# The start of a two-stage layer kernel: batch one's step size on another engine, its state weights in other tiles, and a new order of the queues

## The reference

```
x = layernorm(x + mixer(x));  x = layernorm(x + experts(x))
mixer:   z = x Wz;  B, C, dt_raw, X = split(x Win);  delta = softplus(dt_raw + dt_bias)
         h_t = exp(-delta_t exp(A_log)) h_{t-1} + X_t (delta_t B_t);   y_t = h_t C_t + D X_t
         out = (y * (silu(z) Wzg)) Wout              # 8 heads of 64, state size 64
experts: three routers x P_w^T U_r^T, top 3 of 12, softmax -> dw1, dw2, dw3
         h = gelu(sum_e dw1[e] W1[e] x);  y = sum_e dw2[e] W2[e] h + dw3 b2
```

## Time and profile before

| | |
|---|---|
| median of three runs | 1564.96 us (1563.9 to 1566.89) |
| the profiled execution | 1565.38 us |
| its span | 1563.7 us |
| TensorE busy | 1545.0 us, 99% |
| VectorE, ScalarE, POOL busy | 1108.0, 598.1, 663.7 us |
| chain of waits, by engine | TensorE 92%, POOL 4%, the rest 1% and less |
| DMA | 114.79 MB |

### The profile page before, as it was taken

One profiled execution on the slowest core, in us unless ns is written; L12 is line 12 of the kernel. 1 busy time (PEld: TensorE's weight loads), 2 busy tenths in 40 slices (PEclk: granted clock), 3 DMA queues, 4 the chain that ended last, 5 costly groups with the idle time before them and its releaser, 6 DMA issues.

```text
span 1563.7 us, 25298 instructions
## 1 busy us (share of the span) xinstructions
PE 1545.0 (99%) x8634; PEld 1249.2 (80%) x8634; DVE 1108.0 (71%) x3108; ACT 598.1 (38%) x1362; POOL 663.7 (42%) x755
## 2 busy tenths in 40 slices
PE   8999999999999999999999999999999999999998
PEld 6778788888888878888788888878888788887876
DVE  7577676877768687676776768777686776867755
ACT  6652424425144351533425244242443515335130
POOL 7681623616145270643616336162451715436040
PEclk9999999999999999999999999999999999999999
DMA  5350312304023040321403123040230403214020
GB/s 176 102 158 22 116 41 66 98 29 132 19 76 88 29 135 14 103 69 46 118 17 118 44 66 98 29 128 22 71 93 29 136 14 99 73 40 125 15 74 7
DMA packets 81600, 114.79 MB, mean 73 GB/s; under 512 B 10160, under 2 KB 37312, under 8 KB 81472
## 3 DMA queue, kind: packets, MB, share of 16 engines
q1 hardware_dynamic: 81472, 113.18, 24.9%
HBM read 108.02 MB, written 5.13 MB: 72 GB/s over the span
## 4 chain that ended last, share of the span: by engine, by line
PE 92%; POOL 4%; issue 1%; DVE 1%; DMA 1%; ACT 0%; SPq 0%; POOLq 0%; DVEq 0%; ACTq 0%
PE exp_bank L246 22%; PE exp_bank L248 22%; PE exp_bank L247 22%; PE mix_bank L893 4%; PE mix_bank L919 3%; PE mix_bank L246 3%; PE mix_bank L247 3%; PE mix_bank L248 3%; PE mix_bank L901 3%; PE mix_bank L790 1%; PE turn_bank L1224 1%; POOL w_lo L445 1%; PE mix_bank L738 1%; POOL Wt L853 1%; PE mix_bank L1010 1%
## 5 line engine op out<-in xcount | busy, mean ns | idle before, releaser
L1167 POOL TENSOR_TENSOR sp_lo<-fbuf,sp_hi 128x512 fp32r<-128x512 f32 (+2 forms) x203 | 246.6, 1218 | 179.3 <-ACT sp_hi L1164 112.7
L246 PE MATMUL exp_bank<-w_hi,sp_hi 128*128 128x512 f32 x768 | 307.5, 400 | 0.8 <-POOL sp_lo L1217 0.8
L246 PE MATMUL exp_bank<-sp_hi,w_hi 128*128 128x512 f32 x764 | 304.9, 399 | 2.2 <-POOL sp_lo L1167 2.0
L248 PE MATMUL exp_bank<-w_hi,sp_lo 128*128 128x512 f32 x768 | 303.2, 395 | 0.0
L247 PE MATMUL exp_bank<-w_lo,sp_hi 128*128 128x512 f32 x768 | 303.1, 395 | 0.0
L248 PE MATMUL exp_bank<-sp_hi,w_lo 128*128 128x512 f32 x764 | 300.5, 393 | 0.0
L247 PE MATMUL exp_bank<-sp_lo,w_hi 128*128 128x512 f32 x764 | 298.8, 391 | 0.0
L1264 DVE SCALAR_TENSOR_TENSOR acc<-exp_bank,dw,acc 128x128 f32<-128x128 f32 x384 | 132.2, 344 | 152.9 <-PE exp_bank L248 152.2
L1164 ACT CAST sp_hi<-fbuf 128x512 fp32r<-128x512 f32 (+2 forms) x203 | 120.0, 591 | 277.2 <-DVE fbuf L1134 217.2
L853 POOL TENSOR_TENSOR Wt<-Wt,Gh 128x512 f32<-128x512 f32 x128 | 184.9, 1446 | 23.0 <-DVE Wt L845 22.9
L246 PEld LDWEIGHTS exp_bank<-sp_hi,w_hi 128*128 128x128 f32 x764 | 143.6, 188 | 43.2 <-issue 8.0
(11 more groups left out here) (267 smaller groups left out, 2281.4 us busy)
## 6 DMA issues: line engine op xcount, KB each, us to landing
row_b<-dw_rows SPq DMA_DIRECT2D x190, 256.0 KB, 3.4
seg_b<-dA_rows SPq DMA_DIRECT2D x124, 256.0 KB, 3.6
ctd<-cum_rows SPq DMA_DIRECT2D x128, 96.0 KB, 3.3
x_in<-in_x SPq DMA_DIRECT2D x16, 256.0 KB, 2.8
result<-acc SPq DMA_DIRECT2D x15, 256.0 KB, 2.3
fbuf<-in_W1T SPq DMA_DIRECT2D x12, 256.0 KB, 4.2
acc<-in_W2T SPq DMA_DIRECT2D x5, 256.0 KB, 4.0
x_in<-in_W2T SPq DMA_DIRECT2D x3, 256.0 KB, 4.4
```

What stands on the lines that cost most here:

```text
L246: nc.tensor.matmul(ps, s_hi, m_hi, start=start and j == 0, stop=False)
L248: last = nc.tensor.matmul(ps, s_lo, m_hi, start=False, stop=stop and j == n - 1)
L1167: sig("xw_lo", PO.tensor_tensor(lo[:, cols], wide[e % 2][:, cols], hi[:, cols].bitcast(F32), ALU.subtract))
```

## The change

All of it lies in the setup, in the start and in the functions that they call. What it does:

- Batch one's step size (mix_step) runs on VectorE, in two halves with the mask copies between; the unit copy into PSUM moves from VectorE to ScalarE, ahead of everything. wzg_lo is made before the silu products.
- Batch one's state weights lie in zg (Xde0) instead of Wt. Its scans wait for the silu rests and the unit copy and no longer for the state matmuls; the copy of the first gate tile waits for the state matmuls instead.
- Batch two's xT_lo moves from VectorE to POOL. TensorE transposes batch two's x before batch one's scores.
- Weights: tiles 0 and 1 are cast on ScalarE, and their rests taken on VectorE later; tiles 2 and 3 get their rests on POOL, after a wait for the first ctd product. The others move in the queues of ScalarE and POOL, and their loads in that of SP.
- SP sends the rates, waits for that to land, reads rows 0 and 1, and only then sends the cumulative product.
- Batch two's step size: its first half on POOL comes before three rests of weights and its second half after them; its reciprocal on VectorE comes after the residual sum (L924) instead of before the last gate product; on ScalarE it comes after the tanh.
- VectorE's normalisation waits for the weights up to tile 8, ScalarE's x1T for those up to tile 9, and the logits copy for all twelve.
- TensorE: the rates of batch one come before X2 and X3; the states after the first gate tile; batch two's dt matmuls after y of the second pair; 29 filler matmuls fewer.

```
-        N1, NHP, LO_V = 12, 2, (0, 1, 2, 3)
+        N1, LO_V = 12, (0, 1)
@@ mix_x
-            if eng is DVE:
-                wait(DVE, "xT", b)
...
+            if eng is (PO if early else DVE):
+                wait(eng, "xT", b)
@@ mix_decay
-                wait(DVE, "ps_st", b)
+                if first(b):
+                    DVE.wait_ge(sems["unit"], 1)
+                    wait(DVE, "silu_lo", b)
+                else:
+                    wait(DVE, "ps_st", b)
@@ start_pe
-            mix_X(PE, b, range(4))
+            mix_X(PE, b, range(2))
...
             mix_rates(PE, b)
             mix_ends(PE, b)
+            mix_X(PE, b, range(2, 4))
+            mix_x(PE, nxt, True)
             router_product(PE)
-            keep_busy(rb, 6)
             mix_scores(PE, b)
-            keep_busy(rb, 12)
-            mix_states(PE, b)
-            mix_x(PE, nxt, True)
...
-            mix_zg(PE, b)
+            mix_zg(PE, b, range(1))
+            mix_states(PE, b)
+            mix_zg(PE, b, range(1, 3))
             mix_y_skip(PE, b, 0)
             mix_y(PE, b, 0)
             mix_y_skip(PE, b, 1)
+            mix_zg(PE, b, [3])
+            mix_y(PE, b, 1)
             mix_dt(PE, nxt)
-            mix_y(PE, b, 1)
+            mix_y_skip(PE, b, 2)
             mix_bc(PE, nxt)
-            mix_y_skip(PE, b, 2)
             mix_y(PE, b, 2)
             mix_z(PE, nxt)
             mix_y_skip(PE, b, 3)
             mix_y(PE, b, 3)
-            keep_busy(rb, 6)
+            keep_busy(rb, 3)
             mix_out(PE, b)
             mix_X(PE, nxt, range(2))
-            keep_busy(rb, 14)
+            keep_busy(rb, 6)
@@ start_dve
+            mix_step(DVE, b, on=DVE, parts=(0,))
             setup_masks(DVE)
-            split_w(DVE, range(0, 2))
-            mix_step(DVE, b)
+            mix_step(DVE, b, on=DVE, parts=(1,))
+            setup_zg(DVE)
             mix_z(DVE, b)
-            mix_X(DVE, b, range(2))
-            mix_silu_split(DVE, b, on=DVE)
+            mix_X(DVE, b, range(3))
             DVE.wait_ge(sems["zero"], 16)
             mix_rates(DVE, b)
-            setup_zg(DVE)
-            mix_X(DVE, b, range(2, 4))
-            split_w(DVE, range(2, 4))
+            mix_silu_split(DVE, b, on=DVE)
+            mix_X(DVE, b, [3])
             router_product(DVE)
+            split_w(DVE, range(2))
...
-            mix_step(DVE, nxt)
             mix_y(DVE, b, NQ - 1)
             mix_z(DVE, nxt)
             mix_out(DVE, b)
+            mix_step(DVE, nxt)
             route_stats(DVE, b)
+            first_weights_ready(DVE, 8)
+            route_scale(DVE, b)
             first_weights_ready(DVE)
-            route_scale(DVE, b)
@@ start_pool
-            neg_a_ready(PO)
-            mix_step(PO, b)
+            PO.wait_ge(sems["cast"], NCAST)
             skip_tables(PO)
             mix_ends(PO, b)
-            split_w(PO, range(4, 6))
             for q in range(NQ):
                 mix_decay(PO, b, 2 * q)
                 mix_decay(PO, b, 2 * q + 1)
-                if 0 < q < NQ - 1:
-                    split_w(PO, [5 + q])
-            mix_step(PO, nxt)
-            split_w(PO, range(8, 12))
+                if q == 0:
+                    wait(PO, "ctd", b, 1)
+                split_w(PO, ([2, 3], [4], [5], [])[q])
+                if q == 0:
+                    mix_x(PO, nxt, True)
+            mix_step(PO, nxt, parts=(0,))
+            split_w(PO, range(6, 9))
+            mix_step(PO, nxt, parts=(1,))
+            split_w(PO, [9])
             load_b2(PO)
             wait(PO, "x1", b)
+            split_w(PO, range(10, 12))
```

More of the change, by code:

```diff
@@ L349, in setup @@
                 AC.preload_act_table_set(LOG_EXP)
+                AC.wait_ge(sems["ident"], 2)
+                AC.copy(unit[:, :], ident4[:, :]).then_inc(sems["unit"], 1)
                 AC.wait_ge(sems["pad"], 5)
@@ L433, in split_w @@
                 at, landed, n = w_stage(k)
-                if k < NHP:
-                    if eng is DVE:
[L436 to L439, removed]
+                if eng is AC:
                     AC.wait_ge(landed, n)
@@ L531, in mix_dt @@
                 wait(AC, "ps_st", b.prev())
-                AC.copy(B_tok[:, :, :], ps[:, :, 0:NS])
-                wait(AC, "G_dt", b.prev())
+                if not first(b):
+                    AC.copy(B_tok[:, :, :], ps[:, :, 0:NS])
+                    wait(AC, "G_dt", b.prev())
                 sig("dt_raw", AC.copy(delta[:, :, :], ps[:, :, NS:NS + H]))
+                if first(b):
+                    AC.copy(B_tok[:, :, :], ps[:, :, 0:NS]).then_inc(sems["B_first"], 1)
         def mix_step(eng, b, on=PO, table=True, parts=(0, 1)):
@@ L615, in out_rows, with mix_z @@
                 out[bass.ds(b.index(), 1), :, :].rearrange("o (c p) d -> p (o c) d", p=P)
[L617 to L619 removed]
+        def mix_z(eng, b, ks=range(NK)):
+            for k in ks:
                 if eng is PE:
@@ L667, in mix_zg @@
                     wait(AC, "ps_out", b.prev())
+                    if first(b):
+                        wait(AC, "ps_st", b)
                     sig("zg", AC.copy(zg[:, q, :], bank_of(f"zg{q}", b)[:, :]))
@@ L749, in mix_ends @@
                 ps = bank_of("rates", b)
-                for part, first in ((a_hi, True), (a_lo, False)):
+                for part, opens in ((a_hi, True), (a_lo, False)):
                     PE.matmul(ps[:, P:P + (NC - 1) * H], strict_r[:, :], part[:, 0:NC - 1, :].rearrange("p c h -> p (c h)"),
-                              start=first, stop=not first)
+                              start=opens, stop=not opens)
                 sig("ps_ends", PE.matmul(ps[:, P + 64:P + 64 + NC * H], upper[:, P - 1:P].to_broadcast([P, P]),
@@ L1530, in start_act @@
             mix_ends(AC, b)
+            mix_silu_split(AC, b, on=DVE)
             mix_bc(AC, b)
-            split_w(AC, range(2, 6))
+            split_w(AC, range(2))
             mix_scores(AC, b)
```

83 lines of the change are left out of this document (46 added, 37 removed).

## The result

| | before | after |
|---|---|---|
| median of 20 runs each, in turns | 1565.45 us (1562.72 to 1567.41) | 1567.55 us (1564.26 to 1571.98) |
| ratio after to before | | 1.0018, 95% interval 1.001 to 1.0026 |
| profiled execution, its span | 1565.38, 1563.7 us | 1564.99, 1563.3 us |

The changed kernel is slower by about 2 us, and its median lies outside the range of 1560.6 to 1565.3. Two facts have to be held apart. The execution that was profiled is as long as the one of before; and the executions of the changed kernel do not agree with each other. Of its 20, ten took 1564.3 to 1566.9 us at a mean granted clock of 0.994 to 0.996, and ten 1568.2 to 1572.0 us at 0.991 to 0.993. The profile shows one of the first ten.

A forecast was written before the change was run, and what follows sets the result against it. POOL's chain from 9 to 57 us was taken to set the first expert matmul's start; 1.9 us earlier plus 0.4 of clock made 2.3, so 1563.1 from 1565.38 (1562.7 from the median), range 1560.6 to 1565.3.

The forecast's parts named there:

- Steps 1 to 5: From batch one's step size to the normalised x: gate 1.75 us earlier, residual sum done at 52.0, normalised x 2.2 earlier.
- step 1: Batch one's step size on VectorE, at 0.3 us an operation: done at 14.4 us, 3.0 before POOL's 17.46.
- Step 3: First ctd at 29.4; POOL waits for it, then takes rests and x rest: only 0.5 of 2.6 us left.
- Step 5: Gate at 46.75, 1.75 us earlier; residual sum at 52.0; L960's wait falls by 0.8, so normalised x comes 2.2 earlier.
- step 2: VectorE up to the first scan, weight and silu rests charged 1.8 and 1.9 beside POOL: scan at 23.8, 2.6 us earlier.
- Step 6: POOL's rests end at 59.8 and release the logits copy, 1.5 us earlier; ScalarE's copy of G ends 1.9 earlier.
- Step 7: Low-clock stretch comes earlier, over logits and scores, hidden by POOL's 59.8; the X matmul gets back 0.4 us.
- rival B: The new 3.2 us TensorE hole before y of the second pair costs 1.7 us of clock: 1564.4; chance 0.2.
- C: Rival: same hole, clock low until the last y; over the whole 10.8 us costs 5.4, 1568.1 us; chance 0.08.
- D: Rival: gain lost behind 72 us if late weights do not move with the rest: 1565.0 us; chance 0.07.
- A: Rival: less collision on VectorE than charged, cheaper rests and steps, whole 0.7 of clock back: 1561.4 us; chance 0.25.

The follow-up runs named there:

- a_nine: Changed kernel with measured fillers, reciprocal ahead of the residual sum, and tile 9's rest on VectorE instead of POOL; 1562.46 us, ratio to before 0.9979.
- a_tuned: Changed kernel with fillers measured to its holes (10, 2, 11, 18 and 3), reciprocal left behind the residual sum; 1563.78 us, ratio to before 0.9986.
- b_fill: Kernel before with fillers measured to its own holes (11, 3, 9, 18 and 3), nothing of the change; 1563.08 us, ratio to before 0.9985.
- a_r12: a_tuned with POOL's rests of tiles 12 and 13 taken in only 4 of 512 columns; 1562.57 us, ratio to before 0.9984.
- a_again: The changed kernel itself, run again without any edit; 1569.98 us, ratio to before 1.0022.
- a_hole11: Changed kernel with 11 fillers in the hole before y of the second pair, no other edit; 1565.76 us, ratio to before 1.0.
- a_late: Changed kernel with the earlier fillers around the output product given back (6 and 14 instead of 3 and 6); 1566.96 us, ratio to before 0.9999.

## Why the prediction was wrong

**Steps 1 to 5, up to the residual sum: right as a whole.** Predicted and measured, in us: a_lo 14.4 and 14.16; first scan 23.8 and 23.13; first ctd 29.4 and 29.15; y of the second pair done 37.8 and 37.73; gate 46.75 and 46.88; residual sum done 52.0 and 52.19. The two weight rests beside POOL cost 2.27 (L439), 0.5 more than the 1.8 charged, and the pair of silu rests, also beside POOL's state weights, 1.26 instead of 1.9, so not every such overlap stalls VectorE; POOL's tables took 2.03 instead of 3.74 and its state weights 4.86 instead of at most 4.0. That these errors cancel is luck. The steps had a pitch of 0.3 as taken (0.19 of it work for most); the lower bound of step 1 adds up to 12.3 and not 12.8, which changes nothing. Step 3's claim, that of a scan 2.6 us earlier little arrives because POOL takes on the x rest, holds: the scan came 3.3 earlier, y of the second pair 1.2.

**Step 5, the normalisation, mis-sized.** L975 started at 55.27, as forecast (57.57 - 2.2 = 55.4). But L975 was carried over at its 1.11 us, with POOL's rest of tile 9 newly beside it: 2.44. The prediction named that POOL's tiles would follow the reciprocal and asked only who waits for their end, not who runs beside them. It had charged exactly this at step 2, from the rests of the earlier trace rows, and left it out here. In a_nine the collision is worth 0.8 us.

**Step 6, "POOL decides again": right only at an even clock, and short in range.** POOL's last rest of the first set ended at 60.31 instead of 59.8. In the profile after, the logits matmuls ended later than that (61.10), as they ran at 1.2 GHz, and it was they that released the copy; POOL's rest released only ScalarE's cast of a late tile, at 60.34. The same eight took 1.1 us before. The group of TensorE's logits matmuls, 56 to 62 us:

```profile
L1019 PE MATMUL exp_bank<-router,fbuf 128*128 128x36 f32 x8 | 1.9, 410 | 0.8 <-ACT fbuf L1011 0.8
```

With the clock up (a_tuned) they end in time and the copy starts at 60.40, when POOL is done. Behind that, step 6 took "a stretch that had 8.4 us" over unchanged. That is the largest single term of the even-clock sum: the stretch from the logits copy to the first expert matmul grew from 9.54 us (b_fill) to 10.54 (a_tuned), because the rests of tiles 12 and 13 fall on the comparisons: with them short (a_r12) it is 9.63.

**Step 7, the clock: failed, and it decides the sign.** The prediction let the late low stretch move to where POOL hides it and give back 0.4. It came earlier (58.5 against 61.1), but lasted twice as long (6.8 against 3.4 us), over logits, scores and the first X. The early low stretch (14.2 to 21.1) was not foreseen; it was hidden behind VectorE, whose first scan starts at 23.13 with it and at 23.14 without (a_tuned). And the hole before the second pair's y, to which the sum gave nothing and rival B one stretch of 3.4 us with a chance of 0.2, costs 3.1 us at the last y in the profile of a_again. That about half of the first 20 executions fell there is inferred from their times. Rival B compared two holes of one profiled execution, and held it against the risk that TensorE stood from 11.9 to 14.9 at a granted 1.00. In the profile after, it stood 2.38 us in that place, up to 14.41, and the clock fell at 14.2, in a_again only at 16.0. So a hole can cost in one execution and not in the next, and one profile cannot show that.

**The rivals.** B named the place, and its price was for half the low time found; C's mechanism, a low clock until near the last y, is nearer: 36.6 to 43.4, about 60% of its 10.8 us. The executions of the slower kind took 1568.2 to 1572.0, at or above its 1568.1; that the median of all, 1567.55, comes so near to C's price is luck, for it lies between two kinds. Both together had 0.28, and the slower side only 0.04. The Trainium skill (TensorE: Matmul & The Clock Gate, HAM oscillation) states that idle gaps put the array back to half rate each time anew; the runs agree for three of the five profiles with this hole unfilled, and for the late one in every profile that had the change's few fillers there. D is refuted: from the first expert matmul to the end of the span it is 1491.7 us before and 1490.8 after, and 1490.0 to 1492.7 in all the kernels here. A is refuted too: there was more collision, not less.

**The sum, with what the runs showed in its place:** a lead of 1.9 us at the residual sum (against b_fill; 1.6 against the profile of before, where 1.8 was forecast), less 0.6 at the normalisation, less 0.1 at the logits, less 1.0 in the routing, leaves 0.2 at even clock. On top of that the change opens holes which cost it some 4 us (1567.55 against 1563.78 with all of them filled), where the holes of the kernel before cost 2.4 (1565.51 against 1563.08). The difference of the two is the result. By place, the middle hole alone is worth 1.8 to 2.8 us (a_hole11) and the late ones alone 3.0 (a_late against a_again); these are of different groups of runs and need not add up to the whole.

## What to carry to other kernels

When work moves from a saturated helper engine to another, list what will then run beside each short operation on the path, and charge every one of them up to a whole instruction of the other engine. Where a change drops filler or makes a new wait on TensorE, measure several executions of it and compare their mean clocks before believing the profile of one; and before pricing any change near a hole, fill the holes of the kernel before, which here alone was worth as much as the change was meant to bring.

## What the runs showed that was not expected

- The granted clock after one and the same hole of 2.69 us stayed at 1.00 in one execution of a kernel and went to 0.50 in another. The low stretches seen lasted 3.4 us (61.1 to 64.6 before), 6.8 (14.2 to 21.1 and 58.5 to 65.4 after, 36.6 to 43.4 in a_again) and 10.2 (60.5 to 70.7 in a_again).
- A VectorE operation of 128x4 elements, 0.16 us elsewhere, stood for 1.16 us until POOL's rest of 1.29 us was over. MAX8 on 128x12, which has one input, did not stall: the twelve of batch one took 0.96 us beside POOL's rests, and all 192 of the kernel before lie between 0.153 and 0.176 us each.
- More work on TensorE made the kernel before faster: 52 matmul records more up to 72 us, 2.4 us less in all.
